# Ternary pieces, table products and layer-norm rows put elsewhere, and a new begin of the experts, in a two-layer gated attention and expert network

## What is computed

```python
x = x + tanh(g_xattn[0]) * L0_xattn(layernorm(x), ctx)    # 16 heads, 4 key/value heads, RMS norm and rotary tables on q and k,
                                                            # 64 context keys per batch, then causal own keys
x = x + tanh(g_ffn[0])   * L0_ffn(layernorm(x))           # shared expert + 16 experts, 4 chosen per token, 256 slots each
x = x + tanh(g_xattn[1]) * L1_xattn(layernorm(x), ctx)    # 8-bit quantised projections
x = x + tanh(g_ffn[1])   * L1_ffn(layernorm(x))           # ternary weights: round(tanh(w / mean|w|)), 8-bit activations
```

## Time and profile before

| what | value |
|---|---|
| median of 3 runs | 1983.78 us (1982.28 to 1983.98) |
| the profiled execution's own time | 1983.36 us |
| its span, first to last instruction | 1981.6 us |
| what lies around the span | 1.8 us |
| PE busy | 93% of the span (DVE 55, ACT 52, POOL 49%) |
| mean granted PE clock | 0.978 of full |

### The profile page before, as it was taken

The page is one execution under the profiler, slowest core; times in us unless marked ns, Lnnn a source line. Parts: engine busy times, 40 slices in busy tenths (PEclk is TensorE's granted clock), DMA queues, the critical chain, the costliest instruction groups (busy, mean ns, idle before and its releaser), DMA issues. The chain is left out here.

```text
span 1981.6 us, 27597 instructions
## 1 busy us (share of the span) xinstructions
PE 1847.4 (93%) x9759; PEld 1324.2 (67%) x9796; DVE 1098.1 (55%) x2264; ACT 1038.0 (52%) x2252; POOL 962.9 (49%) x865
## 2 busy tenths in 40 slices
PE   6999999999999999999997999989999968869998
PEld 4666666776766666766774887769999746644443
DVE  4544544445455654565444648524444567868886
ACT  3555656644544545544444321125656466757775
POOL 4544565444653445554431100007888446657774
PEclk8999999999999999999999999999999979989999
DMA  7111111211012111111010300136888870000000
GB/s 236 45 50 50 48 34 44 66 31 50 34 34 71 49 50 42 30 52 48 2 64 20 109 30 22 43 109 194 241 227 253 220 160 1 1 0 23 22 17 27
DMA packets 112952, 141.18 MB, mean 71 GB/s; under 512 B 37408, under 2 KB 68128, under 8 KB 112624
## 3 DMA queue, kind: packets, MB, share of 16 engines
q1 hardware_dynamic: 105648, 122.63, 19.7%
q0 software_dynamic: 7168, 16.78, 4.0%
HBM read 104.78 MB, written 29.36 MB: 68 GB/s over the span
## 5 line engine op out<-in xcount | busy, mean ns | idle before, releaser
L743 POOL TENSOR_TENSOR a_xcl<-xT,a_xch 128x512 fp32r<-128x512 f32 x64 | 82.4, 1288 | 322.7 <-ACT a_xch L558 322.7
L898 PE MATMUL a_A<-a_pT,a_vf 128*128 128x512 f32 (+1 forms) x448 | 237.2, 611 | 0.9 <-ACT a_pT L574 0.9
L848 PE MATMUL a_S<-a_kT,a_qT 128*128 128x288 f32 (+3 forms) x640 | 210.0, 426 | 4.8 <-ACT a_qT L586 3.1
L659 DVE TENSOR_REDUCE a_nmax<-a_S 128x1 f32<-128x192 f32 (+3 forms) x256 | 138.1, 551 | 85.1 <-PE a_S L849 83.8
L564 ACT ACTIVATE a_pr_odd<-a_S,a_nmax 128x320 f32<-128x320 f32 (+1 forms) x128 | 80.9, 633 | 156.3 <-DVE a_nmax L659 155.1
L120 PE MATMUL a_A<-a_wlo,a_xch 128*128 128x512 f32 x256 | 153.3, 599 | 6.4 <-DVE a_qT L655 6.4
L848 PEld LDWEIGHTS a_S<-a_kT,a_qT 128*128 128x128 f32 x640 | 115.1, 190 | 54.5 <-issue 28.3
L574 ACT ACTIVATE a_pT<-a_TR 128x512 f32<-128x512 f32 (+1 forms) x224 | 132.2, 590 | 34.7 <-PE a_TR L888 33.8
L564 ACT ACTIVATE a_pr_even<-a_S,a_nmax 128x192 f32<-128x192 f32 (+1 forms) x128 | 67.0, 525 | 135.0 <-DVE a_nmax L659 134.9
L1503 POOL TENSOR_TENSOR e_wlo<-expert_raw,e_whi 128x1408 fp32r<-128x1408 f32 x32 | 102.7, 3232 | 66.8 <-ACT e_whi L1673 66.8
L699 DVE TENSOR_TENSOR a_otl<-a_A,a_oth 128x512 fp32r<-128x512 f32 x64 | 44.2, 691 | 152.2 <-ACT a_oth L578 152.2
(11 more groups left out here) (389 smaller groups left out, 5133.6 us busy)
## 6 DMA issues: line engine op xcount, KB each, us to landing
a_pw<-in_L_ffn_w_dram SPq DMA_DIRECT2D x96, 256.0 KB, 2.8
expert_raw<-in_L_ffn_w_gate_dram SPq DMA_DIRECT2D x16, 704.0 KB
expert_raw<-in_L_ffn_w_up_dram SPq DMA_DIRECT2D x16, 704.0 KB
expert_raw<-in_L_ffn_w_down_dram SPq DMA_DIRECT2D x16, 512.0 KB
tern<-a_tern SPq DMA_DIRECT2D x48, 128.0 KB, 1.9
x_res<-in_x_dram SPq DMA_DIRECT2D x4, 1024.0 KB, 9.2
a_raw<-in_L_xattn_wq_dram SPq DMA_DIRECT2D x4, 1024.0 KB, 6.2
a_raw<-in_L_xattn_wo_dram SPq DMA_DIRECT2D x4, 1024.0 KB, 5.4
```

The costliest lines, as they stand in the source:

```text
L659: ve.tensor_reduce(nmax[:, s % 2, i:i + 1], pair(s, i), AX.X, ALU.max, negate=True).then_inc(s_max, 1)
L743: pool.tensor_tensor(xcl[:, t % 2], xT[:, :, tok(t)], xch[:, t % 2].bitcast(F32), ALU.subtract).then_inc(xlo_ready, 1)
L848: pe.matmul(bank[:, lo:hi], qT[:, t % 2, hq], kT[:, par(t), lo:hi], start=True, stop=hi < nk)
L898: last = pe.matmul(A[:, A_USE["V", t, 0][0]], vf[r, par(t), i], pT[r, i % 2], start=i == 0, stop=i == nkt - 1)
```

## The change

Six things change. (1) The drain slot 64 gets lists of its own ("last"): the four row tiles of the next stage are summed, normalised, turned and copied there, no longer in slots 60 to 64; PE turns them into the score banks `S` (which nothing uses any more), and DVE, not ACT, copies them to `xT`. (2) Ternary work leaves slots 33, 34, 49 and 50 and takes slots 56 to 59; in third slots its second piece stands behind the fourth maximum and its scaling. (3) The tables are made in two parts, keys' (t0) ahead of c1, queries' (t1) behind it, each sine product in one operation instead of four. (4) In slot -2 DVE's A goes ahead of E. (5) The front stage of the feed-forward part no longer waits at its end for its stores; SP (at the experts' begin) and POOL (at its first add) wait for them. (6) At the experts' begin DVE, not POOL, makes gate's low half of expert 0, and ACT makes the tokens' high half behind gate's. In POOL's `split_lo` a wait for the count of low halves so far is added for every expert.

```diff
+    PE_ORDER = {"last": "W0 W1 W2 W3 R0 P0 P1 V0 R1 P2 V1 P3 V2 R2 P4 V3 R3 V4", -3: ...
+    ACT_ORDER = {"last": "g0 g1 g2 g3 g4 o L", -3: ...
-                 0: "x e0 j0 e1 g0 j1 v e2 r g1 n g2 j2 e3 g3 k t g4 o f L",
+                 0: "x e0 j0 e1 g0 j1 v e2 r g1 n g2 j2 e3 g3 k t g4 o f",
     DVE_SLOT = "M0 M1 N0 L D X v M2 N1 N2 j0 j1 M3 N3 B E A"
-    DVE_ORDER = {-3: "A0 A1 X0 A2 X1 A3 X2 X3 b u c0 t c1", -2: "v E A", ...
-                 0: DVE_SLOT, 1: DVE_SLOT, 2: DVE_SLOT, 3: DVE_SLOT}
+    DVE_ORDER = {"last": "A0 A1 X0 D X1 r0 A2 X2 r1 A3 X3 r2 r3 B", -3: "A0 A1 X0 A2 X1 A3 X2 X3 b u c0 t0 c1 t1", -2: "v A E", ...
+                 0: DVE_SLOT, 1: DVE_SLOT, 2: "M0 M1 N0 L D X v M2 N1 N2 j0 M3 N3 j1 B E A", 3: DVE_SLOT}
+    POOL_ORDER = {"last": "r0 r1 r2 r3", -3: ...
...
-    TERN_SLOTS = [*range(24, 28), *range(32, 44), *range(48, 56)]
+    TERN_SLOTS = [*range(24, 28), 32, *range(35, 44), 48, *range(51, 60)]
...
+                    if name == "r":
+                        t = row(s, 5, i)
+                        ve.wait_ge(xn_turned, t + 1)
+                        ve.wait_ge(xlo_ready, SLOTS)
+                        ve.tensor_copy(xT[:, :, tok(t)], S[:, i].rearrange("p (k t) -> p k t", k=KD)).then_inc(xT_ready, 1)
...
-                        for q, wr in (("k", kw[:]), ("q", wrow[:, 0])):
...
-                            for t in range(BT):
-                                ve.tensor_tensor(sw[q][:, t], sw["q"][:, t], swapped, ALU.mult).then_inc(tab_ready, 1)
+                        q, wr = (("k", kw[:]), ("q", wrow[:, 0]))[i]
...
+                        ve.tensor_tensor(sw[q][:], sw["q"][:], swapped, ALU.mult).then_inc(tab_ready, 1)
...
                         pe.wait_ge(xn_ready, t + 1)
-                        bank = bank_of_TR("R", t, 0, s, m)
+                        if s == SLOTS:
+                            pe.wait_ge(s_exp, GH * SLOTS)
+                            bank = S[:, i]
+                        else:
+                            bank = bank_of_TR("R", t, 0, s, m)
...
-                for r in range(RING):
-                    sp.wait_ge(stored[r], 16 * (NT - BT) // RING)
-                sp.wait_ge(y_stored, 16 * (NT + 2 * NS))
...
             @block.sync
             def _(sp):
+                sp.wait_ge(y_stored, 16 * (NT + 2 * NS))
                 for e in range(2, E):
...
                 def split_lo(e):
-                    for j in range(2):
+
+                    for j in (1,) if e == 0 else range(2):
                         pool.wait_ge(whi_ready, NW * e + j + 1)
+                        pool.wait_ge(gu_lo, 2 * e + j)
...
+                    else:
+                        pool.wait_ge(y_stored, 16 * (NT + 2 * NS))
...
-                for j in range(NW):
+                split_hi(0, 0)
+                split_x(0)
+                for j in range(1, NW):
                     split_hi(0, j)
-                split_x(0)
...
+                ve.wait_ge(whi_ready, 1)
+                for q, cs in pieces(0):
+                    ve.tensor_tensor(wlo[0][q, cs], raw[q, 0, cs], whi[0][q, cs].bitcast(F32), ALU.subtract).then_inc(gu_lo, 1)
                 split_x(0)
                 split_down(0)
```

More of the change, by code:

```diff
@@ L126, in attention0_stage @@
                      consts, kctx_dram, vctx_dram, ffn_in, tern_dram, total_dram, mean):
-    PE_ORDER = {-3: "Z0 Z1 R0 R1 R2 R3 C0 C1",
+    PE_ORDER = {"last": "W0 W1 W2 W3 R0 P0 P1 V0 R1 P2 V1 P3 V2 R2 P4 V3 R3 V4", -3: "Z0 Z1 R0 R1 R2 R3 C0 C1",
                 -2: "k0 k1 q0 q1 H0 q2 q3 H1",
@@ L140, in attention0_stage @@
                 3: "S0 W0 W1 S1 W2 W3 P0 k0 k1 S2 R P1 V0 q0 P2 V1 S3 P3 K V2 q1 T V3 q2 q3"}
-    ACT_ORDER = {-3: "z0 z1 r0 r1 r2 r3 x u w c0",
+    ACT_ORDER = {"last": "g0 g1 g2 g3 g4 o L", -3: "z0 z1 r0 r1 r2 r3 x u w c0",
                  -2: "c1 x v h0 f h1",
@@ L154, in attention0_stage @@
     DVE_SLOT = "M0 M1 N0 L D X v M2 N1 N2 j0 j1 M3 N3 B E A"
-    DVE_ORDER = {-3: "A0 A1 X0 A2 X1 A3 X2 X3 b u c0 t c1", -2: "v E A", -1: "v X E A", "first": DVE_SLOT,
-                 0: DVE_SLOT, 1: DVE_SLOT, 2: DVE_SLOT, 3: DVE_SLOT}
-    POOL_ORDER = {-3: "r0 r1 r2 r3 x w c0", -2: "x c1 r", -1: "q x r", "first": "x q p0 p1 r",
+    DVE_ORDER = {"last": "A0 A1 X0 D X1 r0 A2 X2 r1 A3 X3 r2 r3 B", -3: "A0 A1 X0 A2 X1 A3 X2 X3 b u c0 t0 c1 t1", -2: "v A E", -1: "v X E A", "first": DVE_SLOT,
+                 0: DVE_SLOT, 1: DVE_SLOT, 2: "M0 M1 N0 L D X v M2 N1 N2 j0 M3 N3 j1 B E A", 3: DVE_SLOT}
+    POOL_ORDER = {"last": "r0 r1 r2 r3", -3: "r0 r1 r2 r3 x w c0", -2: "x c1 r", -1: "q x r", "first": "x q p0 p1 r",
                   0: "x q p0 p1 r", 1: "x q p0 u p1 w r", 2: "w q x p0 p1 r", 3: "x q p0 p1 r"}
@@ L174, in steps @@
     def steps(order, s):
-        return [(word[0], int(word[1:] or 0)) for word in order[s if s < 0 else s % BT if s > 0 else "first"].split()]
+        kind = s if s < 0 else "first" if s == 0 else "last" if s == SLOTS else s % BT
+        return [(word[0], int(word[1:] or 0)) for word in order[kind].split()]
     def batch_next(s):
@@ L184, in row @@
             return i
-        n = s + ahead
-        return n if BT <= n < PERIOD else n - AGAIN if PERIOD <= n - AGAIN < PERIOD + BT else None
+        if s == SLOTS:
+            return PERIOD + i
+        return s + ahead if BT <= s + ahead < PERIOD else None
     def bank_order(firsts):
@@ L197, in bank_order @@
                 elif name == "R":
-                    if row(s, 5, i) is not None:
+                    if s < SLOTS and row(s, 5, i) is not None:
                         taken.append((name, row(s, 5, i), 0))
@@ L509, in do @@
                                        ACT.Copy).then_inc(ctx_copied, 1)
-                    if name == "r" and row(s, 5, i) is not None:
+                    if name == "r" and s < SLOTS and row(s, 5, i) is not None:
                         t = row(s, 5, i)
                         act.wait_ge(xn_turned, t + 1)
-                        if t >= PERIOD:
-                            act.wait_ge(xlo_ready, SLOTS)
                         act.activation(xT[:, :, tok(t)], TR[:, TR_USE["R", t, 0][0]].rearrange("p (k t) -> p k t", k=KD),
@@ L1413, in load_expert, with experts_stage @@
     sp.dma_start(d[0:I - full, EXPERT_TILES - 1], wd[full:I]).then_inc(loaded, 16)
-def experts_stage(nc, ident, xn_dram, y_dram, wg_in, wu_in, wd_in, raw, loaded, ids, slot_weight, xg, gathered, eo, added, load_next,
+def experts_stage(nc, ident, xn_dram, y_dram, y_stored, wg_in, wu_in, wd_in, raw, loaded, ids, slot_weight, xg, gathered, eo, added, load_next,
                   homes, attention, x, mean, at, gates, mask_in, att_loaded, x_loaded):
@@ L2471, in build @@
         bridge, kept = ctx.enter_context(ExitStack()), ctx.enter_context(ExitStack())
-        added = ctx.enter_context(nc.semaphore("expert_added"))
+        added, y_stored = ctx.enter_context(nc.semaphore("expert_added")), ctx.enter_context(nc.semaphore("y_stored"))
         att_loaded = [ctx.enter_context(nc.semaphore(f"att_loaded{j}")) for j in range(6)]
@@ L2519, in build @@
             attention = (wT, sq, gsw, mask, kbd, vbd, ctx_raw, bk, bv, bq, gbo, amax, sw, inv, ident_h, scalars)
-            experts_stage(nc, ident, xn_dram, y_dram, *weights, raw, loaded, ids, slot_weight, xg, gathered, eo, added, load_attention1,
+            experts_stage(nc, ident, xn_dram, y_dram, y_stored, *weights, raw, loaded, ids, slot_weight, xg, gathered, eo, added, load_attention1,
                           homes, attention, x, mean, at, gates, a["mask_BxSxS2_ff0"], att_loaded, x_loaded)
```

26 lines of the change are left out of this document (14 added, 12 removed).

## The result

The changed kernel takes 1953.64 us (median of 4 runs, 1952.09 to 1954.13), the kernel before 1983.18 (1982.28 to 1983.98): ratio 0.9851, 95% interval [0.9835, 0.9866]. The forecast was 1957.5 us, range 1950 to 1966. The profiled execution took 1953.28 us, its span 1951.5 us where before's was 1981.6, at a mean granted clock of 0.985 (before 0.978).

The account below looks back on a forecast made before the run. PE, the busiest engine, bounds the kernel; time is gained where it waits or runs at half clock afterwards. Terms 7.8 + 7.5 + 4.4 + 3.0 + 3.2 = 25.9 us, from 1983.36, gave 1957.5 us; range 1950 to 1966.

Parts of the forecast that it names:

- Front, 7.8 us: Front: second H 4.5 us earlier, PE's waits of 0.96 and 2.32 us gone; ends 5 and 9.5 us.
- So 29.7 now: Front: POOL's norm of the context keys, no longer waiting 1.08 us for DVE, lets second H start at 29.7, before 34.25.
- rival of the front: Front: queries' tables run beside POOL's work and hold E up as before; 3 of 7.8 us remain, 1962; chance 0.10.
- Slots 33, 34, 49, 50, 7.5 us: These slots, without ternary work beside POOL's halving, gain 4.5 + 3.0 us; ends 5.5 and 8.1.
- Third slots, 4 x 1.11 = 4.4 us: Slots 26, 38, 42, 54: second piece behind the fourth maximum, 16.41 to 15.30 us each; ends 2.2 and 4.4.
- signs of being wrong: Would refute the forecast: POOL without idle time in an expert, first S later than 44, pieces lengthening slots 56 to 59.
- rival of the second piece: Five slots: the piece behind the fourth maximum delays B and next W by what it saved; 1962 or 1963; chance 0.03.
- Last slots, 3.0 us: Slots 61 to 63 lose a turn each, slot 62 its 1.47 us wait; slot 64 costs nothing; ends 0 and 4.5.
- rival of the last slot: Slot 64: two tiles 1 to 2 us late each, B behind them; 3.0 becomes 0 or -1, 1961; chance 0.07.
- Experts' begin, 3.2 us: Experts' begin: stage starts near 1329.7, gate at 1333.9 instead of 1337.72, up's low half late next; ends 1.9 and 4.5.
- The half clock elsewhere: Whole kernel: earlier waits move half-clock stretches; two more or less give 1961 or 1954 us; chance 0.15.
- POOL the bound: Experts: the added wait in `split_lo` makes POOL the limit, slower, 1997 us with one whole halving; chance 0.03.

Follow-up runs that it names:

- first experiment: The kernel after with both tables ahead of c1 again in DVE's begin, all else unchanged: 1956.52 us, ratio 0.9874.
- second four experiments: A group of four follow-up runs on variants of the kernel after; ratios are against 7 runs of before on the same chip. The text does not list the four.

## Why the prediction was right

- **Front, 7.8 us.** The steps held in kind: q starts 3.6 us earlier, and both waits behind H are gone. The size is 7.9 to 8.4 us against before (40.32 less 31.9 to 32.5) in the seven further profiles that have after's front, none with half clock on k, and 6.7 in the one shown. That it fits is in part luck, for two steps inside it failed and offset each other. "So 29.7 now" for the second H measured 30.5 to 30.8, a loss of about 1 us: I let POOL's norm of the context keys begin when DVE's sums are there, but it begins behind POOL's own halving, first norm and step x, and its product ended at 30.78 where before it ended at 30.74. In the first profile step x took 1.74 us beside DVE's q tables; in two runs of the same front it took 1.28, but there the halving had taken 6.8 to 6.9 us instead of 6.1, and H1 came no earlier. So PE stands up to 2.1 us ahead of H1, a wait that I had not named. The other step is the way from H1 to the first S: 14.41 us before, less the two waits, makes 11.1, and at full clock it measured 9.7. Of the 1.4 us more, 1.1 lie between K and the first S (5.43 us before, 4.36 now), where half clock stood behind the 2.32 us wait (43.6 to 47.0 us before); that it goes with the wait I had only as an upper end.
- **Front, q and the tables.** The sum's q at full clock held in some runs and not in others; where it did not, q hid it ahead of the wait for H1. Of the 3.6 us by which q starts earlier, the order of the tables is 1.3 (first experiment); in the first S it is worth nothing that is shown apart from the clock. The rival of the front falls all the same: the queries' tables did run beside POOL (1.52 and 1.31 us instead of 0.68 and 0.21), but E no longer held PE.
- **A ahead of E.** Shown by its undoing: the 2.3 us wait is back, and half clock behind it.
- **Slots 33, 34, 49, 50, 7.5 us.** Measured 8.1: nothing stayed of the 0.28 us a pair that I took, in the middle between slot 18 and a slot without work. Slot 18's 0.56 us is a late first W (1.35 us into the slot, 0.78 in slots 34 and 50 of after), and without a pair in slot 33 or 49 there is none. 1.5 of the 8.1 is slot 34's half clock. That slots 56 to 59 cost nothing held for 56, 57 and 59.
- **Third slots, 4 x 1.11 = 4.4 us.** Mis-sized: 3.6, and slot 58 paid 0.2 where I wrote that it stays (a piece lengthening slots 56 to 59 was among my signs of being wrong). I put the whole 1.11 us to the fourth maximum; 0.87 to 0.9 was, the other 0.2 belongs to the pair in the second slot ahead, which the change leaves. The rival of the second piece falls: no third slot with pieces is longer than 15.52 us, where the rival had 16.4.
- **Last slots, 3.0 us.** 2.9 from the edit. Slot 64 at nothing held to 0.02 us; DVE's chain of sums, normalising and copies was not the limit, and the rival of the last slot falls.
- **Experts' begin, 3.2 us.** 3.6. The stage began 1.8 us earlier instead of 1.6, DVE's low half took 1.63 us (bound 1.8) and up waited 0.39 us, where my working has it 0.5 late (1337.1 against 1333.9 + 2.7; by these the gain is 3.3). Undone in two parts, 1.7 us at the first turn and 2.2 at gate. At the first down product it is 3.6 us with after's first profile and 2.1 with its second, whose half clock there was as long as before's (10.2 us): 1.5 of the 3.6 can go with the clock.
- **The half clock elsewhere.** A rival with 0.15, and it is what came: about 5 us of the 30.1 (slot 1, the shared expert, and in slot 64 a stretch that the edit there does not explain) are half clock that fell elsewhere, and after came again with slot 1 at 16.22. Without them the parts make some 25 us, the forecast 25.9. So the parts bear out the forecast, and the time of 1953.64 us is that rival's 1954, not the forecast's 1957.5. The Trainium skill, page "TensorE: Matmul & The Clock Gate", section "What's actually happening", has the monitor's window run freely; the traces agree: in six profiles of one front with the same wait of 2.63 us ahead of q, the first stretch began at 25.0, 26.4, 26.5 or 30.8 us, or in two of them not ahead of 1060 us.
- **POOL the bound** falls: the added wait costs POOL 0.19 us an expert (0.08 a wait in my working), and it has 0.67 us idle.
- **The range.** The terms' upper ends sum to 31.0 us and not to 29.7, so 1952 and not 1954; the range down to 1950 holds either way.

So part of the measured gain is clock that the change need not keep. Among the seven runs of before that stood beside the second four experiments are two of 1974.92 and 1975.06 us at a mean granted clock of 0.982; the other five, at 0.978, took 1982.27 to 1983.72. From 1974.92 to the lowest time of after, 1952.09, are 22.8 us; from median to median 29.5. No run here tells why the higher clock is granted oftener after the change.

## What to carry to other kernels

Cost an edit in the stage it touches and measure it there, from one event of the engine that bounds it to another: here most of the parts, undone one by one, showed their terms to a few tenths, while the time of the whole hid one of 2 us. Look at where half clock lies in both profiles before a difference is put down to the edit. Work on an idle engine is not free beside a neighbour that shares something with it: look at what the other engine runs at that very moment, and move the work by one step. Don't read spare time out of a profile in which half clock has slowed the engine that hides it.
